# Output projection of an attention and expert block: two fp32 products against three fp32r products of high and low halves

## The chip, the cores and the metric

The kernel runs on one core of one Trainium2 chip. The metric is the device time of one execution in microseconds (us). Before the change it is 2347.66 us, the median of three runs (2343.93 to 2350.57). The engines are named as in the profile: PE is TensorE, PEld its weight loads, DVE VectorE, ACT ScalarE, POOL GpSimd, SP the engine that issues most DMAs.

## The reference

The input x has 16 blocks of 512 rows and 128 columns. The output is x + attention(xn) + experts(xn), where xn is the layer norm of x. The part that the change touches is the attention's last line:

```
new_vals = einsum('bhqk,bkhd->bqhd', softmax(q k^T), v)        # 16 heads of 64
out      = einsum('bqhe,hed->bqd', new_vals, w_out) + b_out
```

The expert part sends each row to the best two of 8 experts, each a two-layer network with silu, and adds the weighted results. Everything is in fp32, or as exact as three fp32r products of high and low halves make it.

## The kernel before, in words

All work is cut into groups G = 0, 1, 2, ... (256 that attend, and 6 more at the end). A pair of heads n (128 pairs: 16 blocks x 8) takes two groups, 2n and 2n+1: in each, PE makes the scores of two of its four row tiles (line 349), DVE takes the negated row maximum (line 355), ACT the exponential with its sum (line 360). One group later PE turns these tiles (line 372, four times four transposes) and DVE and ACT copy them from PSUM to PT (lines 384 and 382). In the middle of the four turns PE makes the next pair's K product (even groups) or Q product (odd groups), each as three fp32r products (helper `three`, lines 200 to 202); ACT casts its high half from PSUM (line 334) and DVE subtracts for the low half (line 335).

The later steps of a pair n are these. In group 2n+2 DVE takes the reciprocal of the row sums (line 406), PE turns it (line 411, called R below), DVE copies it (line 413) and two DMAs on SP write it to memory and read it back as the broadcast RB. In group 2n+3, as its last PE work, `weighted` makes the product with V (line 395, called PV), and DVE multiplies the result by RB into OT (line 401). In group 2n+4, for odd n, `project_out` multiplies the heads of the pairs n-1 and n by their parts of the output weights (lines 427 and 428, called OP), and DVE adds the result into acc (line 436). OT has four buffers. These OP groups are the ones with G%4 == 2; those with G%4 == 0 have two V products for the same or the next block in that place instead (`values`). After them in a group come R and the side work: the router of a block in the first half of the run (`router`, `logits`, `routed_rows` on POOL, and so on), and one expert tile in each three groups in the second half (from G = 138).

Order. Every engine runs its own queue, in an order fixed while the program is written: `add` puts an instruction with the names it needs into the group's open list, and `close` sorts DVE's and ACT's list by place. In DVE's list a group's places are max0, turn0, inverse, max1, low, turn1 and then everything else (side). In ACT's they are exp00, turn0, high, exp01, exp10, turn1, exp11, side. PE, POOL and SP keep the order in which the code adds.

Banks. Two pairs of PSUM banks hold the scores. Four more rotate (`xbank`), one for each other product in PE's order, and each use waits for the instruction that emptied the bank four uses earlier (`freed`). So in every group the third turned tile's bank, the K or Q product's bank and so on come back in a fixed rhythm.

The weights of the K, Q, V and router products are split into halves at the start by `split_weights` (ACT casts the high half, POOL or DVE subtracts). The output weights come by one DMA, whole, in fp32. RAW is a staging buffer for expert weights; its first use is in group 24.

Of the kernel before, what the change touches and what calls it, by code (L numbers as in the profile page):

```python
# [8 lines left out]
F32R = mybir.dt.float32r  # L9
# [6 lines left out]
P = 128  # L16
D = 128
# [12 lines left out]
WSPLIT = 24  # L30
DVE_ORDER = "max0 turn0 inverse max1 low turn1 side".split()
ACT_ORDER = "exp00 turn0 high exp01 exp10 turn1 exp11 side".split()
KQ_AT = 2
# [40 lines left out]
def block_kernel(nc, x, wq, wk, wv, wout, ns, bout, rw1, rb1, rw2, rb2, w1, w2, bias, ident, tri, consts, pick, out):  # L74
# [11 lines left out]
    with ExitStack() as ctx:  # L86
        def sb(name, shape, dt=F32, to=ctx):
            return to.enter_context(nc.sbuf_tensor(name, shape, dt))
# [10 lines left out]
        WV = sb("WV", [P, 2, H * DH], F32R)  # L99
        WO = sb("WO", [P, HP, D])  # L100
        RB2 = sb("RB2", [P, 1])
# [23 lines left out]
        RB = sb("RB", [P, 2, S])  # L125
        OT = sb("OT", [P, 4, S])
        acc = sb("acc", [P, QT, D])
# [89 lines left out]
        def stage_raw(n):  # L217
            src = (w1 if n < E else w2)[:, n % E * 512:(n % E + 1) * 512]
            add("sp", lambda e: e.dma_start(RAW[:, n % 2], src), needs=[("slo", n - 2)] if n >= 2 else [],
                name=("raw", n), step=16, sem=f"raw_{n % 2}")  # L220
# [166 lines left out]
        def weighted(n):  # L387
            b, p = divmod(n, HP)
            bk = xbank()

            def make(e):
                for k in range(QT):
                    for j in range(2):
                        h = 2 * p + j
                        m = e.matmul(bank[bk][j * DH:(j + 1) * DH, :], V[:, k, h * DH:(h + 1) * DH],  # L395
                                     PT[:, n % 2 * 2 + j, k, :], start=(k == 0), stop=(k == QT - 1))
                return m

            add("pe", make, needs=[("PT", n, QT - 1, 0), ("PT", n, QT - 1, 1), ("Vs", b, p // 4, QT - 1), ("Vs", b, p // 4, QT - 2),
                                   freed.get(bk)], name=("PV", n))  # L400
            add("dve", lambda e: e.tensor_tensor(OT[:, n % 4, :], bank[bk], RB[:, n % 2, :], ALU.mult),  # L401
                needs=[("PV", n), ("RB", n), ("OP", (n - 4) | 1) if n >= 4 else None], name=("OT", n))
            freed[bk] = ("OT", n)
# [5 lines left out]
        def spread(n):  # L409
# [10 lines left out]
                needs=[("rrow", n), ("OT", n - 2) if n >= 2 else None], name=("RB", n), step=16, sem=f"RB_{n % 2}")  # L420

        def project_out(n):
            b, p = divmod(n, HP)
            bk = xbank()

            def make(e):
                e.matmul(bank[bk], WO[:, p - 1, :], OT[:, (n - 1) % 4, :], start=True, stop=False)  # L427
                return e.matmul(bank[bk], WO[:, p, :], OT[:, n % 4, :], start=False, stop=True)  # L428

            add("pe", make, needs=[("OT", n), ("load", "wo"), freed.get(bk)], name=("OP", n))  # L430
            dst = acc[:].rearrange("p t d -> p (t d)")
# [345 lines left out]
        load("tri", TRI[:], tri)  # L777
        load("wo", WO[:].rearrange("p a b -> p (a b)"), wout)
        load("bo", BO[:], bout)
# [27 lines left out]
        split_weights("wq", wq_s, WQ, [1], DH ** -0.5, on="dve")  # L807
        split_weights("r1", r1_s, R1, [0])
        add("dve", lambda e: e.tensor_scalar(RB1H[:], RB1[:], 0.5, None, ALU.mult), needs=[("load", "rb1")], name=("rb1h",))
        add("dve", lambda e: e.memset(PM[:, 0, 0], 0.0), name=("pm0",))  # L810
# [136 lines left out]
        def group(G):  # L947
# [16 lines left out]
            if G % 2 == 0 and 1 <= G <= GROUPS:  # L964
                denominators(G // 2 - 1)
            halves_after(G)
            attending(G)
            if G % 2 == 0 and 1 <= G <= GROUPS:
# [86 lines left out]
```

How the kernel before makes its waits and increments, by code:

```python
    def emit(self, engine, eng, sems):  # L62
        seen = {}
        for make, needs, key, step in self.items[engine]:
            for sem, value in (self.value[n] for n in needs):
                if seen.get(sem, 0) < value:
                    eng.wait_ge(sems[sem], value)
                    seen[sem] = value
            ins = make(eng)
            if key is not None:
                ins.then_inc(sems[key], step)
# [915 lines left out]
        @block.sync  # L987
        def _(eng):
            q.emit("sp", eng, sems)
            for k, v in q.count.items():
                if k.startswith(("st_", "sadd", "spare_out", "base", "rrow", "tab", "b_tab", "sc_", "pads")):
                    eng.wait_ge(sems[k], v)
```

## Time and profile before

| | |
|---|---|
| median of three runs | 2347.66 us |
| the profiled execution's own time | 2347.15 us |
| its span, first to last instruction | 2345.3 us |
| mean granted TensorE clock | 0.983 of full speed |
| ACT busy | 1453.1 us (62%) |
| POOL busy | 952.1 us (41%) |
| line 427, OT by WO, 128 passes | 68.2 us busy |
| line 428, OT by WO, 128 passes | 66.4 us busy |
| line 401, OT, 128 | 88.1 us busy, 688 ns each |

How to read it: each of the 64 OPs has two fp32 matmuls, and each shows as two passes, so 256 passes in the two lines. A matmul's record is longer than the time until the next one may start, since matmuls are pipelined; the distance between starts is what PE spends. The same holds to a lesser degree for DVE and ACT. A wait is put down to the engine and line that came last.

### The profile page before, as it was taken

What the parts mean: (1) busy time and instruction counts of PE and PEld (TensorE: products, weight loads), DVE (VectorE), ACT (ScalarE), POOL (GpSimd) and SP (SyncE); (2) the same over time, 40 slices, a digit from 0 to 9 for tenths busy, and PEclk for the clock granted to TensorE, in tenths of its full rate; (3) what the DMA queues carried; (4) which work ended last, traced back from release to release, by engine and by line L of the source; (5) the groups of instructions that cost most, each with busy time, mean ns of one, the idle gap of its engine ahead of it and who ended that gap; (6) DMA issues with size and microseconds to landing.
All of it is one profiled execution on the core that took longest, in us unless ns stands there. A gap on an engine that the chain in (4) does not pass through costs nothing.

```text
span 2345.3 us, 36846 instructions
## 1 busy us (share of the span) xinstructions
PE 2199.6 (94%) x12720; PEld 1395.6 (60%) x12720; DVE 1752.8 (75%) x2908; ACT 1453.1 (62%) x3455; POOL 952.1 (41%) x793
## 2 busy tenths in 40 slices
PE   8999999999999999997999998999989989999997
PEld 5666566656666666654656665565656655656654
DVE  6777777777778878775777776777767767777775
ACT  5666666666666666654665665666666656666663
POOL 5333343544343433310145445445454354454353
PEclk8999999999999999998999999999999999999999
DMA  2122222211111010003133333323233223232232
GB/s 73 34 64 78 85 80 82 91 46 34 37 37 35 27 42 33 29 31 89 37 69 73 73 70 59 71 69 76 69 72 73 59 56 73 69 73 69 66 67 46
DMA packets 126856, 141.67 MB, mean 60 GB/s; under 512 B 18480, under 2 KB 93104, under 8 KB 126640
## 3 DMA queue, kind: packets, MB, share of 16 engines
q1 hardware_dynamic: 96080, 118.60, 16.2%
q0 software_dynamic: 30592, 20.73, 7.2%
q8 instruction: 102, 1.67, 0.3%
q14 instruction: 82, 0.67, 0.1%
HBM read 102.92 MB, written 38.46 MB: 60 GB/s over the span
## 4 chain that ended last, share of the span: by engine, by line
PE 47%; DVE 21%; DMA 12%; ACT 9%; issue 7%; POOL 2%; DVEq 0%; SPq 0%; ACTq 0%; POOLq 0%
PE bank L395 14%; PE pair L349 10%; DMA RB<-l_rows 9%; PE bank L372 8%; DVE NM L355 7%; DVE PT L384 3%; ACT PR L360 3%; DVE ZZ L709 2%; PE bank L427 2%; PE bank L428 2%; PE bank L200 2%; DMA l_rows<-RT 2%; ACT PT L382 2%; PE bank L720 2%; DVE QS L335 1%
## 5 line engine op out<-in xcount | busy, mean ns | idle before, releaser
L360 ACT ACTIVATE PR<-pair,NM 128x512 f32<-128x512 f32 x1024 | 715.0, 706 | 707.5 <-DVE NM L355 706.3
L355 DVE TENSOR_REDUCE NM<-pair 128x2 f32<-128x1024 f32 x512 | 617.3, 1206 | 135.2 <-PE pair L349 134.8
L372 PE MATMUL bank<-idn,PR 128*128 128x128 f32 x4096 | 560.7, 279 | 34.8 <-DVE PT L384 16.6
L372 PEld LDWEIGHTS bank<-idn,PR 128*128 128x128 f32 x4096 | 460.2, 142 | 181.5 <-issue 86.0
L395 PE MATMUL bank<-PT,V 128*64 128x512 f32 x2048 | 469.4, 600 | 15.4 <-ACT ZZ L700 8.7
L712 POOL TENSOR_TENSOR HH<-ZZ,HH 128x512 fp32r<-128x512 f32 x156 | 231.7, 1494 | 572.2 <-DVE HH L711 572.2
L349 PE MATMUL pair<-KS,QS 64*128 64x512 f32 x3072 | 435.6, 415 | 2.1 <-DVE QS L335 1.1
L349 PEld LDWEIGHTS pair<-KS,QS 64*128 64x128 f32 x3072 | 273.8, 187 | 190.1 <-issue 137.1
L384 DVE COPY PT<-bank 128x512 f32<-128x512 f32 x512 | 349.9, 683 | 18.5 <-PE bank L372 10.8
L382 ACT COPY PT<-bank 128x512 f32<-128x512 f32 x512 | 302.9, 592 | 8.5 <-PE bank L372 8.5
L395 PEld LDWEIGHTS bank<-PT,V 128*64 128x64 f32 x2048 | 136.2, 137 | 276.7 <-issue 230.6
L751 POOL DMA_INDIRECT out<-YS,IDW x156 | 245.0, 1571 | 71.1 <-issue 34.2
L489 POOL TENSOR_TENSOR TH<-TH,HS 128x512 f32<-128x512 f32 x64 | 82.2, 1285 | 460.0 <-ACT HS L486 459.7
L401 DVE TENSOR_TENSOR OT<-bank,RB 128x512 f32<-128x512 f32 x128 | 88.1, 688 | 239.9 <-PE bank L395 156.5
L360 ACT ACTIVATION_READ_ACCUMULATOR PR<-pair,NM 128x1 f32 x1024 | 221.7, 216 | 0.0
L592 POOL DMA_INDIRECT slots<-XR,IDX x128 | 124.7, 974 | 106.1 <-DVE junk L587 71.8
L709 DVE SCALAR_TENSOR_TENSOR ZZ<-ZT,ZZ 128x512 f32<-128x512 f32 x156 | 107.2, 687 | 76.6 <-ACT ZZ L700 76.4
L698 ACT ACTIVATE ZT<-bank,BT 128x512 f32<-128x512 f32 x156 | 110.6, 709 | 56.3 <-POOL HH L712 53.3
L711 DVE CAST HH<-ZZ 128x512 fp32r<-128x512 f32 x156 | 138.0, 884 | 5.4
L700 ACT ACTIVATE ZZ<-bank,BT 128x512 f32<-128x512 f32 x156 | 111.0, 711 | 0.0
L335 DVE TENSOR_TENSOR QS<-bank,QS 128x512 fp32r<-128x512 f32 x128 | 88.5, 691 | 16.3 <-ACT QS L334 13.9
L335 DVE TENSOR_TENSOR KS<-bank,KS 128x512 fp32r<-128x512 f32 x128 | 87.7, 685 | 14.8 <-ACT KS L334 14.4
(164 smaller groups left out, 2866.4 us busy)
## 6 DMA issues: line engine op xcount, KB each, us to landing
E<-w_tab SPq DMA_DIRECT2D x78, 512.0 KB, 7.3
RB<-l_rows SPq DMA_DIRECT2D x128, 256.0 KB
XG<-slots SPq DMA_DIRECT2D x39, 264.0 KB, 7.4
w_tab<-SPL SPq DMA_DIRECT2D x16, 512.0 KB, 4.8
xin<-in_x SPq DMA_DIRECT2D x16, 256.0 KB, 7.7
XQ<-in_x SPq DMA_DIRECT2D x16, 256.0 KB, 6.9
RAW<-in_w SPq DMA_DIRECT2D x16, 256.0 KB, 7.9
slots<-PAD SPq DMA_DIRECT2D x15, 264.0 KB, 5.1
```

The source lines that it names most:

```text
L335: add("dve", lambda e: e.tensor_tensor(lo, bank[bk], hi, ALU.subtract), needs=[(name + "hi", n), *old], name=(name + "lo", n), place="low")
L349: m = e.matmul(bank[bk + j], a[half[j], cols], c[half[j], :], start=(k == 0), stop=(k == 2))
L355: add("dve", lambda e: e.tensor_reduce(NM[:, 2 * t:2 * t + 2], pairs[t % 2][:], AX.X, ALU.max, negate=True), needs=[("S", n, t), ("exp", n ...
L360: add("act", lambda e: e.activation(PR[:, k, :], bank[t % 2 * 2 + j], ACT.Exp, bias=NM[:, k:k + 1], accum_out=RS[:, n % 2, j, t:t + 1]), n ...
L372: m = e.transpose(bank[bk][:, c * P:(c + 1) * P], PR[:, k, c * P:(c + 1) * P], idn[:])
L382: add("act", lambda e: e.copy(dst, src), needs=[("T", n, t, j), *old], name=("PT", n, t, j), place=f"turn{t % 2}")
L384: add("dve", lambda e: e.tensor_copy(dst, src), needs=[("T", n, t, j), *old], name=("PT", n, t, j), place=f"turn{t % 2}")
L395: m = e.matmul(bank[bk][j * DH:(j + 1) * DH, :], V[:, k, h * DH:(h + 1) * DH], PT[:, n % 2 * 2 + j, k, :], start=(k == 0), stop=(k == QT - 1))
L709: add("dve", lambda e: e.scalar_tensor_tensor(ZZ[:, r], ZT[:, r], 1.0, ZZ[:, r], ALU.add, ALU.mult), needs=[("zt", n), ("zz", n)], name=(" ...
L711: add("dve", lambda e: e.tensor_copy(hi, ZZ[:, r]), needs=[("s", n), old], name=("hi", n))
L712: add("pool", lambda e: e.tensor_tensor(lo, ZZ[:, r], hi, ALU.subtract), needs=[("hi", n), old], name=("lo", n))
L751: add("pool", lambda e, t=t: e.indirect_dma_start(out, bass.IndirectOffsetOnAxis(ap=IDW[:, i % 4, t, 0:1].bitcast(U32), axis=0), YS[:, i % ...
```

## The change

The output weights WO and the normalised heads OT are each kept as a high fp32r half and a low half (the rest). The heads now go from PSUM to an fp32 buffer OF, of which there is one; then ACT casts the high half and DVE subtracts for the low half (`halve_heads`), at new places called heads: first in ACT's order and between inverse and max1 in DVE's. Both run in group 2n+4, in every even group. OT has two buffers for each half. An OP is six fp32r matmuls (low weights by high heads, high by high, high by low, for each of two pairs) where it was two fp32 matmuls. The weights come by two DMAs into RAW at the start and are split there by ACT and POOL; the first two expert weights wait for that before they use RAW.

```diff
-DVE_ORDER = "max0 turn0 inverse max1 low turn1 side".split()
-ACT_ORDER = "exp00 turn0 high exp01 exp10 turn1 exp11 side".split()
+DVE_ORDER = "max0 turn0 inverse heads max1 low turn1 side".split()
+ACT_ORDER = "heads exp00 turn0 high exp01 exp10 turn1 exp11 side".split()
...
-        WO = sb("WO", [P, HP, D])
+        WO = sb("WO", [P, 2, HP * D], F32R)
...
-        OT = sb("OT", [P, 4, S])
+        OF = sb("OF", [P, S])
+        OT = sb("OT", [P, 2, 2, S], F32R)
...
-            add("sp", lambda e: e.dma_start(RAW[:, n % 2], src), needs=[("slo", n - 2)] if n >= 2 else [],
+            add("sp", lambda e: e.dma_start(RAW[:, n % 2], src), needs=[("slo", n - 2) if n >= 2 else ("wlo", "wo", n)],
...
-            add("dve", lambda e: e.tensor_tensor(OT[:, n % 4, :], bank[bk], RB[:, n % 2, :], ALU.mult),
-                needs=[("PV", n), ("RB", n), ("OP", (n - 4) | 1) if n >= 4 else None], name=("OT", n))
+            add("dve", lambda e: e.tensor_tensor(OF[:], bank[bk], RB[:, n % 2, :], ALU.mult),
+                needs=[("PV", n), ("RB", n), ("OTl", n - 1) if n else None], name=("OT", n))
...
+        def halve_heads(n):
+            old = [("OP", (n - 2) | 1)] if n >= 2 else []
+            add("act", lambda e: e.copy(OT[:, n % 2, 0], OF[:]), needs=[("OT", n), *old], name=("OTh", n), place="heads")
+            add("dve", lambda e: e.tensor_tensor(OT[:, n % 2, 1], OF[:], OT[:, n % 2, 0], ALU.subtract),
+                needs=[("OTh", n), *old], name=("OTl", n), place="heads")
...
-                e.matmul(bank[bk], WO[:, p - 1, :], OT[:, (n - 1) % 4, :], start=True, stop=False)
-                return e.matmul(bank[bk], WO[:, p, :], OT[:, n % 4, :], start=False, stop=True)
-
-            add("pe", make, needs=[("OT", n), ("load", "wo"), freed.get(bk)], name=("OP", n))
+                for k in (p - 1, p):
+                    hi, lo = OT[:, k % 2, 0], OT[:, k % 2, 1]
+                    wh, wl = (WO[:, j, k * D:(k + 1) * D] for j in range(2))
+                    e.matmul(bank[bk], wl, hi, start=(k < p), stop=False)
+                    e.matmul(bank[bk], wh, hi, start=False, stop=False)
+                    m = e.matmul(bank[bk], wh, lo, start=False, stop=(k == p))
+                return m
+
+            add("pe", make, needs=[("OTl", n), ("wlo", "wo", 0), ("wlo", "wo", 1), freed.get(bk)], name=("OP", n))
...
-        load("wo", WO[:].rearrange("p a b -> p (a b)"), wout)
+        for c in range(2):
+            load(f"wo{c}", RAW[:, c], wout[:, c * 512:(c + 1) * 512])
...
+        split_weights("wo", RAW[:].rearrange("p a b -> p (a b)"), WO, [0, 1])
...
+            if G % 2 == 0 and 0 <= G - 4 < GROUPS:
+                halve_heads(G // 2 - 2)
             attending(G)
```

## Rows read from the trace of the kernel before

**Rows 1.** The page's part 1, busy time of each engine over the whole span.
```profile
PE 2199.6 (94%) x12720; PEld 1395.6 (60%) x12720; DVE 1752.8 (75%) x2908; ACT 1453.1 (62%) x3455; POOL 952.1 (41%) x793
```

**Rows 2.** The page's part 4, shares of the chain that ended last.
```profile
PE 47%; DVE 21%; DMA 12%; ACT 9%; issue 7%; POOL 2%; DVEq 0%; SPq 0%; ACTq 0%; POOLq 0%
```

**Rows 3.** Who waited for whom, whole span: us in total, times, longest us.
```profile
ACT PR L360 <- DVE NM L355: 706.3, 214, 6.4
...
DVE OT L401 <- DMA RB<-l_rows: 83.4, 39, 8.5
...
PEld bank L200 <- DVE KS L335: 31.0, 64, 1.9
...
PEld pair L349 <- ACT PR L360: 7.8, 21, 1.3
```

**Rows 4.** Timeline, routing half, G%4 == 2: start us, duration us, engine, line.
```profile
608.17 1.67 PE L349 MATMUL pair<-KS,QS 64*128 64x512 f32 x12
...
610.45 0.69 ACT L360 ACTIVATE PR<-pair,NM 128x512 f32<-128x512 f32 x1 [4.76 <-DVE NM L355]
...
611.07 0.19 DVE L406 RECIPROCAL RI<-RS 128x8 f32<-128x8 f32 x1
...
612.27 1.02 PE L427 MATMUL bank<-OT,WO 128*128 128x512 f32 x2
612.27 0.68 DVE L335 TENSOR_TENSOR KS<-bank,KS 128x512 fp32r<-128x512 f32 x1
...
612.87 0.68 DVE L384 COPY PT<-bank 128x512 f32<-128x512 f32 x1
...
613.99 0.27 PE L411 MATMUL bank<-idn,RI 128*8 128x128 f32 x1
...
614.02 0.47 PE L200 MATMUL bank<-XT,R 128*128 128x512 f32 x1
...
614.19 0.69 DVE L436 TENSOR_TENSOR acc<-bank,acc 128x512 f32<-128x512 f32 x1 [0.64 <-PE bank L428]
...
614.33 0.39 PE L201 MATMUL bank<-XT,R 128*128 128x512 f32 x1
...
614.56 0.40 PE L202 MATMUL bank<-XT,R 128*128 128x512 f32 x1
...
624.75 0.69 DVE L401 TENSOR_TENSOR OT<-bank,RB 128x512 f32<-128x512 f32 x1 [1.58 <-DMA RB<-l_rows]
```

**Rows 5.** Instructions of lines 225, 709 and 579: ns min/median/max, first and last start us.
```profile
L225 ACT CAST SPL<-RAW x16: 632/638/680, 234.1 to 474.9; 128x512 fp32r<-128x512 f32 x16
```
```profile
L709 DVE SCALAR_TENSOR_TENSOR ZZ<-ZT,ZZ x156: 678/688/693, 1133.5 to 2305.7; 128x512 f32<-128x512 f32 x156
```
```profile
L579 DVE TENSOR_TENSOR gt<-gt x32: 179/188/1194, 94.6 to 1044.6; 128x32 f32<-128x32 f32 x32
```

**Rows 6.** Timeline, routing half, a group with G%4 == 0.
```profile
177.36 1.04 POOL L265 TENSOR_TENSOR XR<-XR,sqo 128x512 f32<-128x512 f32 x1
...
178.14 0.19 DVE L406 RECIPROCAL RI<-RS 128x8 f32<-128x8 f32 x1
...
179.43 0.69 DVE L335 TENSOR_TENSOR KS<-bank,KS 128x512 fp32r<-128x512 f32 x1
...
180.18 0.50 PE L200 MATMUL bank<-WV,HT 128*128 128x512 f32 x1 [0.25 <-DVE KS L335]
...
181.19 1.83 PE L349 MATMUL pair<-KS,QS 64*128 64x512 f32 x12
```

**Rows 7.** Timeline, expert half, a group with G%4 == 2.
```profile
1700.62 0.68 DVE L384 COPY PT<-bank 128x512 f32<-128x512 f32 x1
...
1701.67 0.48 PE L720 MATMUL bank<-HH,E 128*128 128x512 f32 x1
```

**Rows 8.** Timeline, the last output projection of the run.
```profile
2334.96 0.69 DVE L401 TENSOR_TENSOR OT<-bank,RB 128x512 f32<-128x512 f32 x1 [8.47 <-DMA RB<-l_rows]
...
2335.71 2.08 PE L427 MATMUL bank<-OT,WO 128*128 128x512 f32 x2 [6.21 <-DVE OT L401]
```

## The prediction, made before the changed kernel was run

> **What bounds the kernel now.** I read the page's busy shares first, then its chain of waits, then the totals of who waited for whom, then a few microseconds of the timeline in each kind of group.
>
> TensorE (PE) is busy 94% of the span and VectorE (DVE) 75% [rows 1]. The chain that ended last is 47% PE and still 21% DVE [rows 2]. So PE leads, but at some place in each round it is let go by DVE. The waits name the place: the weight load of line 200 (a V product) waited 64 times for DVE's KS, the low half of K that line 335 writes [rows 3]. ScalarE (ACT) is the loose engine: it waited 706.3 us in 214 pieces for the row maximum [rows 3].
>
> The groups G come in fours. In those with G%4 == 2 PE's order after the score products is T, T, K product, T, T, output projection (OP), R (the small turn of the inverse sums), then the next stage's product. In those with G%4 == 0 it is T, T, K product, T, T, V product, V product, R. Four banks rotate, so the second V product takes the K product's bank, which line 335 empties; after an OP it is R that takes that bank, and the product behind R takes the bank of the third T, which a DVE copy (line 384) empties. That copy is DVE's next instruction behind line 335.
>
> **Part by part.**
>
> *The OP on PE.* Today its two fp32 products are four passes. The first starts at 612.27 and R at 613.99: 1.72 us [rows 4]. Three fp32r products of the same width start at 614.02, 614.33 and 614.56, so 0.31 us for the first of a block and 0.23 us for each later one [rows 4]. Six of them take 0.31 + 5 x 0.23 = 1.46 us. PE is given 0.26 us per OP, 64 x 0.26 = 16.6 us in all, if nothing else holds it. No new bank is taken.
>
> *The cast on ACT.* 128 casts at the head of each even group. The nearest row, an fp32r copy from SBUF, has 638 ns [rows 5]. It waits for OT, which stands on DVE just before the first maximum. ACT is idle there for 4.76 us in the sample group, waiting for that maximum [rows 4], and the maximum takes 1.2 us behind OT. The cast ends first; behind it on ACT stands only the exponential that waits for that same maximum. Its cost is 0. Were ACT late, it would be 0.6 us per even group (up to 77 us); the 706.3 us of waits say it is not.
>
> *The subtraction on DVE.* 128 of them, put between the reciprocal and the second maximum in every even group. Its row is bounded by the 688 ns of a 512-wide operation with two SBUF inputs [rows 5], but instructions of DVE overlap a little: line 335 starts at 612.27 and line 384 behind it at 612.87 [rows 4]. So one more in the stream costs 0.60 us. From there on the second maximum, line 335 and line 384 are all 0.60 us later. What each does to PE:
>
> - G%4 == 0: line 335 ends at 179.43 + 0.69 = 180.12 and the V product starts at 180.18, released by it [rows 6]. That wait is there in each such group (64 in [rows 3]); no slack. 62 groups with two V products and the new subtraction x 0.60 = 37.2 us on PE. Everything behind it (R, the scores of the next group) moves along, and DVE's side work is late by the same 0.60, so nothing later takes it back, with two exceptions below.
> - G%4 == 2: R has slack, for line 335 ends at 612.95 and R starts at 613.99. The product behind R doesn't have enough: the copy of line 384 ends at 613.55, the product starts at 614.02 [rows 4]; with the 0.06 us that a release takes it could start at 613.61. With the copy at 614.15 it starts at 614.21, 0.19 late, though OP ended early. In a group of the expert stage the copy ends at 1701.30 and the product starts at 1701.67 [rows 7]; there it comes 0.29 late. So OP's 0.26 us are given away to a wait for the bank, and more: with 31 such groups in each half of the run, 31 x 0.19 + 31 x 0.29 = 14.9 us. DVE's own lateness ends there, since acc waits 0.64 us for OP anyway [rows 4]. The bounds are -0.26 (if the copy isn't late) and +0.60 (if DVE's lateness reaches PE whole).
> - OP itself needs the subtraction's result. It ends some 0.7 us behind the reciprocal (611.26), at 611.95, and OP starts at 612.27 [rows 4]: covered, with 0.3 us left.
>
> *What takes some back.* DVE's OT waited 39 times for the broadcast RB [rows 3], in the routing half as at 624.75, at the start of a G%4 == 0 group [rows 4]. That DMA starts from R's copy in the G%4 == 2 group, behind acc, and these hardly move; so the 0.19 us of that group shorten the wait instead: 31 x 0.19 = -5.9 us. And the scores behind a G%4 == 0 group in the routing half take 1.83 us where others take 1.67 [rows 4, 6], held by the last exponential, 21 times in [rows 3]. ACT slips less than PE, so this bubble closes: 21 x 0.16 = -3.4 us.
>
> *POOL.* The subtraction reads two SBUF tensors. Line 579, a small instruction (128x32) of that kind that often falls beside a POOL tensor operation, has a median of 188 ns and a maximum of 1194 [rows 5]; I read the 1 us more as a wait for such a POOL operation. In the sample group POOL's line 265 runs from 177.36 to 178.40, across the end of the reciprocal at 178.33, and line 266 (as long) follows [rows 6]. This is the group in which routed_rows puts its three POOL tensor operations, 15 in the run. Between 0 and 1.04 us each, taken at the middle: 15 x 0.5 = +7.5 us, on the path, since these are G%4 == 0 groups. In the expert half POOL does indirect DMAs at that place; line 709, two SBUF inputs too, has a maximum of 693 ns in 156 [rows 5], so nothing is added there.
>
> The Trainium skill, "SBUF — State Buffer", section "Who interferes with whom", says that a VectorE instruction with two SBUF inputs contends with a GpSimd one that reads SBUF and that the later of the two is blocked whole. Line 579's maximum agrees [rows 5]. By that rule alone a subtraction that starts just after line 266 would wait all of its 1.04 us, 15.6 us in all in place of 7.5.
>
> *The start.* wout goes as two transfers into RAW, one issue of about 0.5 us more on SP behind everything urgent; two casts more on ACT, two subtractions more on POOL. ACT's first exponential waits for a maximum behind other DVE work, POOL is idle later, and the first user of RAW (the expert weights, G = 24) and of WO (G = 6) are far off. Cost 0, at most 1.2 us (two casts).
>
> *The end.* The last OT starts at 2334.96 behind its DMA and OP at 2335.71 follows at once [rows 8]. Here cast and subtraction stand bare: 0.64 + 0.69 + 0.1 for two releases = 1.4 us. TensorE runs at its lower clock there (two passes 2.08 us, against 0.86 apart in mid run), so OP gives back about 0.5. Net +0.9 us.
>
> **The sum.** 37.2 + 14.9 - 5.9 - 3.4 + 7.5 + 0.9 = +51.2 us. The profiled execution took 2347.15 us (span 2345.3), 0.5 us under the median of the runs shown (2347.66). 2347.15 + 51.2 = 2398.
>
> **Rivals.**
>
> 1. *PE sets the pace and DVE's idle time (2345.3 - 1752.8 = 592.5 us) covers the subtraction* (faster). For it: 94% against 75% [rows 1]. Against it: that idle time lies in front of OT and of the first maximum, not between the reciprocal and line 335, where the 64 waits of line 200 are. Its place is that bank; it decides if the V product's wait for line 335 is under 0.26 us per group on average after the change. Then 64 x -0.26 + 0.9 = -15.7: 2331 us.
> 2. *Half of it.* The G%4 == 2 groups keep OP's 0.26 us (the bank behind R not binding), the others lose 0.60: 37.2 - 16.6 - 3.4 + 0.9 = +18, with POOL's share up to +26: about 2368.
> 3. *DVE is the bound in all even groups:* 0.60 us lost in each of 125: 75 + 7.5 + 0.9 - 3.4 = +80: 2427. For it: chains in the expert half run through five DVE instructions in a row. Against it: acc's wait for OP, in which DVE's lateness ends.
> 4. *The fp32r products of OP don't go at 0.23 us*, the change not doing what it says: at the passes' 0.43 us six take 2.6 us, +0.86 per OP, 55 us on top of 37: about 2440. Against it: every fp32r product in [rows 4].
>
> **How the numbers follow.** Forecast (2398, own range 2380 to 2415) 0.63; rival 3 0.14; rival 2 0.12; rival 1 0.07; rival 4 0.04. The predicted time is 2398. The range takes in rivals 2 and 3 with a little beyond each: 2362 to 2432, leaving out rivals 1 and 4 and some of the tails. About 0.3% (7 us) is what a measurement can tell from no change. Faster 0.07 (rival 1), same 0.04 (the lower end of rival 2), slower 0.89.
>
> **What would show it.** Right: OP to R 1.46 us; the wait of line 200's V product for KS up from 0.5 to about 1.1 us each; a new wait of the product behind R for line 384's copy; ACT's wait for the maximum down by the casts; the subtraction about 0.69 us, over 1 us in some 15 groups. Groups with G%4 == 0 longer by 0.4 to 0.6 us, G%4 == 2 by 0.2 to 0.3, odd ones unchanged. Wrong: an unchanged wait for KS, or even groups no longer than before (rival 1); odd groups longer (rival 3, or ACT as the bound).

## The result

The changed kernel takes 2398.75 us (median of 4 runs, 2396.14 to 2404.33), the kernel before 2349.01 us (median of 4). The ratio is 1.0214, 95% interval 1.0198 to 1.023. The forecast was 2398. The profiled execution took 2396.78 us, its span is 2395.0 us, 49.7 us more than before.

### The profile after

The lines named here are 1 to 12 further down than before: the scores are L350, the maximum L356, the K low half L336, the V product L201, OT is now OF at L402, the cast L425, the subtraction L426, the projection's three products L437 to L439, R L412, acc L448.

The page's busy times and the shares of the chain that ended last (against [rows 1] and [rows 2]):

```profile
PE 2192.8 (92%) x12848; PEld 1424.0 (59%) x12848; DVE 1829.4 (76%) x3036; ACT 1546.4 (65%) x3585; POOL 960.9 (40%) x795
```
```profile
PE 40%; DVE 34%; issue 10%; ACT 8%; DMA 5%; POOL 1%; DVEq 0%; SPq 0%; ACTq 0%; POOLq 0%
```

PE is busy for 7 us less, and DVE's share of the chain has gone from 21% to 34%. That is the whole case in two lines: the engine that got less work isn't the one that lets the groups go.

Who waited for whom (us in total, times, longest), against [rows 3]:

```profile
ACT OT L425 <- DVE OF L402: 357.7, 109, 11.2
ACT PR L361 <- DVE NM L356: 303.4, 227, 6.2
...
PEld bank L201 <- DVE KS L336: 69.3, 64, 2.6
...
DVE OF L402 <- DMA RB<-l_rows: 45.3, 16, 4.2
```

The V product's wait for the K low half is 69.3 us where it was 31.0, in the same 64 places: 0.60 us more in each. ACT's 706.3 us of waiting for the maximum are now split between the cast's wait for OF and the maximum. The wait for RB fell from 83.4 us in 39 places to 45.3 us in 16. Five more waits of the same multiplication, 21.0 us, stand under "issue", with no releaser found; the last of them (9.45 us, below) was put down to RB before (8.47 us). With these five it is 66.3 us in 21 places, a fall of 17 us.

The timeline of the group with G%4 == 2 whose form before is in [rows 4] (start us, duration us, engine, line):

```profile
619.63 1.66 PE L350 MATMUL pair<-KS,QS 64*128 64x512 f32 x12
...
620.47 0.62 ACT L425 CAST OT<-OF 128x512 fp32r<-128x512 f32 x1 [3.33 <-DVE OF L402]
...
621.89 0.69 ACT L361 ACTIVATE PR<-pair,NM 128x512 f32<-128x512 f32 x1 [0.80 <-DVE NM L356]
...
622.62 0.64 DVE L426 TENSOR_TENSOR OT<-OF,OT 128x512 fp32r<-128x512 f32 x1
...
623.18 1.22 DVE L356 TENSOR_REDUCE NM<-pair 128x2 f32<-128x1024 f32 x1
...
623.64 0.48 PE L437 MATMUL bank<-OT,WO 128*128 128x512 f32 x1
...
624.32 0.68 DVE L336 TENSOR_TENSOR KS<-bank,KS 128x512 fp32r<-128x512 f32 x1
...
624.91 0.68 DVE L385 COPY PT<-bank 128x512 f32<-128x512 f32 x1
...
625.15 0.27 PE L412 MATMUL bank<-idn,RI 128*8 128x128 f32 x1
...
625.51 0.68 DVE L448 TENSOR_TENSOR acc<-bank,acc 128x512 f32<-128x512 f32 x1
...
625.65 0.50 PE L201 MATMUL bank<-XT,R 128*128 128x512 f32 x1 [0.24 <-DVE PT L385]
```

The projection takes 625.15 - 623.64 = 1.51 us (1.72 before). But the product behind R (625.65) starts 6.02 us after the scores (619.63), where it was 614.02 - 608.17 = 5.85: 0.17 later. It is let go by L385, whose copy ends at 625.59. PE's saving turned into a wait for a bank. The cast ends at 621.09, ahead of the exponential that waits for the maximum.

A group with G%4 == 0 in the routing half, against [rows 6]:

```profile
180.33 0.62 ACT L425 CAST OT<-OF 128x512 fp32r<-128x512 f32 x1 [3.21 <-DVE OF L402]
...
182.05 0.64 DVE L426 TENSOR_TENSOR OT<-OF,OT 128x512 fp32r<-128x512 f32 x1
...
182.14 1.45 POOL L267 TENSOR_TENSOR XR<-XR,sqo 128x512 f32<-128x512 f32 x1
...
183.74 0.68 DVE L336 TENSOR_TENSOR KS<-bank,KS 128x512 fp32r<-128x512 f32 x1
...
184.47 0.50 PE L201 MATMUL bank<-WV,HT 128*128 128x512 f32 x1 [0.74 <-DVE KS L336]
...
185.47 1.66 PE L350 MATMUL pair<-KS,QS 64*128 64x512 f32 x12
```

PE's idle time ahead of the V product is 0.74 us (0.25 before). POOL's L267 started behind the subtraction and took 1.45 us, where the same operation had taken 1.04: here DVE came first. The scores behind take 1.66 us in place of 1.83, so that bubble closed, as forecast.

The cast and the subtraction over the run (ns min/median/max, first and last start us):

```profile
L425 ACT CAST OT<-OF x128: 615/621/626, 52.1 to 2385.3; 128x512 fp32r<-128x512 f32 x128
```
```profile
L426 DVE TENSOR_TENSOR OT<-OF,OT x128: 632/642/1412, 54.2 to 2385.9; 128x512 fp32r<-128x512 f32 x128
```

The end of the run, against [rows 8]:

```profile
2384.55 0.69 DVE L402 TENSOR_TENSOR OF<-bank,RB 128x512 f32<-128x512 f32 x1 [9.45 <-issue]
...
2385.93 0.69 DVE L426 TENSOR_TENSOR OT<-OF,OT 128x512 fp32r<-128x512 f32 x1 [0.68 <-ACT OT L425]
...
2386.67 0.80 PE L437 MATMUL bank<-OT,WO 128*128 128x512 f32 x1 [8.64 <-DVE OT L426]
...
2389.64 0.69 DVE L448 TENSOR_TENSOR acc<-bank,acc 128x512 f32<-128x512 f32 x1 [3.02 <-PE bank L439]
```

From OF's start to acc's start it takes 5.09 us, where it was 2339.53 - 2334.96 = 4.57 before. Cast and subtraction put 2386.67 - 2384.55 = 2.12 us between OF and the projection (0.75 before), and the projection gives 0.85 us back.

### By kind of group

A group's length is the time from its first score weight load to the next group's, read from each trace. Summed over the routing half (31 groups of each kind, G = 4 to 127) and the expert half (28 or 29 of each, G = 140 to 254), the difference to the kernel before in us:

```
                         routing half, G%4 =       expert half, G%4 =
                          0     1     2     3       0     1     2     3
changed                  +7.5  +1.5  +8.8  +0.1   +11.6  +5.9  +6.5  +2.5
no halving               -2.6  +0.2  -9.3  -0.2    +0.3  +2.9  -8.1  +6.1
no halving, again        -4.4  +0.1 -10.0  -0.1    -0.1  +0.1  -8.1  +9.1
cast only, again         -4.6   0.0  -9.3  -0.2     0.0  +1.5  -7.8 +10.5
fp32 and halving        +15.7  +1.5  +8.2   0.0   +12.9  +5.9 +10.6  -0.1
even pairs late         -12.0  +9.2 +13.7   0.0    +5.6  +4.8  +6.9  +1.6
on POOL                 +10.6   0.0  -9.0  -0.2    -1.3  +2.1 +156.5 -20.9
projection a group later -19.0 +7.7 -22.9 +52.8    +3.4  +5.9 -26.8 +44.4
same, POOL for even     -19.3  +8.9 -23.1 +50.1    -2.4  +3.7 -27.3 +45.9
in DVE's wait           +16.7  +1.6 -27.9  +4.1   +28.4  -5.8 -16.7 +18.2
mixed                    +5.9  +9.5  -5.2  -0.1    +0.2  +1.5  +8.8  +2.6
two subtractions        +46.7 +18.0 +25.1  +6.4   +29.9  +5.5 +27.0  +1.3
```

The changed kernel's line gives 44.4 us; 2.8 lie in the 12 groups between the halves, 1.1 at the end and 1.3 before G = 4.

Not all of this is waiting. The profile shows TensorE's granted clock at its full level (2.4 GHz) through the routing half in both kernels, but at the lower level (1.2 GHz) for 34.1 us of the expert half before the change and for 51.2 us after it. The expert half repeats itself every 12 groups (a tile takes three groups, two pairs take four), and the extra low stretches lie in the groups with G%12 == 4 and the ones behind them. There PE stands idle for a DVE copy, 2.47 or 2.48 us in each of the nine such groups before and 2.75 us after; before, the clock was low somewhere in these two groups in four cases out of nine, after it in all nine. G = 220, before (clock full) and after. The last line is a stretch of the profile; its third number from the end is the granted clock (1.00 is full, 0.50 the lower level). The score products take 2.82 us there in place of 1.66:

```profile
1977.24 0.66 PE L737 MATMUL bank<-idn,YT 128*128 128x128 f32 x4 [2.48 <-DVE V L317]
1977.82 1.66 PE L349 MATMUL pair<-KS,QS 64*128 64x512 f32 x12
```
```profile
2014.73 1.04 PE L749 MATMUL bank<-idn,YT 128*128 128x128 f32 x4 [2.75 <-DVE V L318]
2015.70 2.82 PE L350 MATMUL pair<-KS,QS 64*128 64x512 f32 x12
2014.90:2018.30 3.40, 3.40 (x16) 2.28 (x15) 2.17 (x3) 0.00 (x0) 2.19 (x3) 0.50 0.07 8
```

The nine groups with G%12 == 5 show the price: together they have 13.9 us more at the low level and are 6.2 us longer, 0.45 us for each. That is all of the 5.9 us that the expert half's G%4 == 1 groups grew by, and at this price the half's 17.1 us more are about 8 us (an estimate) of the 49.7. The 1.3 us before G = 4 are of this kind too: in every kernel here that is 1 us or more later at that point, the cast-only ones among them, the clock is low for 3.4 us from about 28 us on, and in no other.

### The profile page after: what moved, and what is told of

The parts are those of the page before. It is cut to its first block, busy times and chain, and to the rows that moved or that the text cites. A ratio compares the mean times of both kernels' runs of the same rounds, so it can differ in the third digit from the quotient of the medians.

```text
span 2395.0 us, 37489 instructions
## 1 busy us (share of the span) xinstructions
PE 2192.8 (92%) x12848; PEld 1424.0 (59%) x12848; DVE 1829.4 (76%) x3036; ACT 1546.4 (65%) x3585; POOL 960.9 (40%) x795
## 4 chain that ended last, share of the span: by engine, by line
PE 40%; DVE 34%; issue 10%; ACT 8%; DMA 5%; POOL 1%; DVEq 0%; SPq 0%; ACTq 0%; POOLq 0%
PE bank L396 14%; PE pair L350 10%; DVE NM L356 10%; DVE PT L385 7%; PE bank L373 5%; DMA RB<-l_rows 4%; DVE ZZ L721 3%; DVE OT L426 3%; DVE KS L336 3%; ACT PR L361 2%; PE bank L732 2%; PE bank L201 2%; DVE HH L723 2%; ACT PT L383 2%; PE bank L734 1%
## 5 line engine op out<-in xcount | busy, mean ns | idle before, releaser
L356 DVE TENSOR_REDUCE NM<-pair 128x2 f32<-128x1024 f32 x512 | 622.6, 1216 | 146.2 <-PE pair L350 145.9
L350 PE MATMUL pair<-KS,QS 64*128 64x512 f32 x3072 | 437.3, 417 | 2.3 <-DVE QS L336 1.2
L350 PEld LDWEIGHTS pair<-KS,QS 64*128 64x128 f32 x3072 | 277.7, 190 | 187.8 <-issue 137.8
L385 DVE COPY PT<-bank 128x512 f32<-128x512 f32 x512 | 349.7, 683 | 18.5 <-PE bank L373 10.5
L425 ACT CAST OT<-OF 128x512 fp32r<-128x512 f32 x128 | 79.5, 621 | 358.0 <-DVE OF L402 357.7
L402 DVE TENSOR_TENSOR OF<-bank,RB 128x512 f32<-128x512 f32 x128 | 88.1, 688 | 230.8 <-PE bank L396 164.5
L361 ACT ACTIVATION_READ_ACCUMULATOR PR<-pair,NM 128x1 f32 x1024 | 215.6, 211 | 0.0
L201 PE MATMUL bank<-WV,HT 128*128 128x512 f32 x128 | 62.8, 491 | 42.6 <-DVE KS L336 41.2
```

The source lines that it names most:

```text
L350: m = e.matmul(bank[bk + j], a[half[j], cols], c[half[j], :], start=(k == 0), stop=(k == 2))
L356: add("dve", lambda e: e.tensor_reduce(NM[:, 2 * t:2 * t + 2], pairs[t % 2][:], AX.X, ALU.max, negate=True), needs=[("S", n, t), ("exp", n ...
L361: add("act", lambda e: e.activation(PR[:, k, :], bank[t % 2 * 2 + j], ACT.Exp, bias=NM[:, k:k + 1], accum_out=RS[:, n % 2, j, t:t + 1]), n ...
L385: add("dve", lambda e: e.tensor_copy(dst, src), needs=[("T", n, t, j), *old], name=("PT", n, t, j), place=f"turn{t % 2}")
```

## The experiments

The theory: DVE's subtraction makes the banks of the K product and of the third turned tile free later, PE waits for these banks, and so even the time that the projection gives back is lost. The rivals: the halving's cost and the projection's gain just add up; DVE's load as such sets the time; the cast is what costs. Ratios are to the kernel before on the same chip, which had medians of 2349.7, 2344.8 and 2345.4 us in the three sets.

### The two parts apart

The changed kernel without any halving:

```diff
-            add("dve", lambda e: e.tensor_tensor(OF[:], bank[bk], RB[:, n % 2, :], ALU.mult),
+            add("dve", lambda e: e.tensor_tensor(OT[:, n % 4, :], bank[bk], RB[:, n % 2, :], ALU.mult),
...
-                    hi, lo = OT[:, k % 2, 0], OT[:, k % 2, 1]
+                    hi, lo = OT[:, (n - p + k) % 4, :], OL[:]
```

> The changed kernel without the halving: the multiplication by RB writes the fp32r heads itself, and the low half of the heads is a tile of zeros, so the third product adds nothing (the low half of the heads is left out of the result). PE does the same six fp32r products. Bank theory: with no subtraction ahead, the projection's shorter time is passed on whole: 64 x 0.21 to 0.26 = 13 to 17 us under before, 2332 to 2337. Rival (PE's time in the projection is hidden anyway, or six weight loads cost something else): 2346 to 2350.

Measured: 2331.67 us, ratio 0.9917 (0.9896 to 0.9939). Again on another chip:

> The kernel without any halving once more, beside the one with the cast alone on the same chip, to price the cast. Expected 0.991 to 0.994 of before.

Measured: 2328.26 us, ratio 0.9928 (0.9912 to 0.9943). The shorter projection is worth 17 to 18 us. In both halves the G%4 == 2 groups are 0.3 us shorter each, but only the routing half keeps it: in the expert half the groups behind them (G%4 == 3) give 6 to 9 us back, and that half as a whole takes 1173.1 and 1172.8 us against 1171.9 before. In the second of the two traces, 3.4 of the 9.1 us lie in the ten groups with G%12 == 11, 0.33 us in nearly each: PE has come there earlier and waits longer for DVE to empty the banks of acc and of a turned tile. 6.6 us lie in two groups (151 and 199) with 10.2 us at the low clock, which had none before. The wait for the K low half is that of before:

```profile
PEld bank L202 <- DVE KS L337: 30.7, 64, 2.2
```

So the rival by which PE's time in the projection is hidden falls.

The kernel before with the halving beside it:

```diff
+            add("act", lambda e: e.copy(OH[:, 0], OT[:, n % 4, :]), ..., name=("OTh", n), place="heads")
+            add("dve", lambda e: e.tensor_tensor(OH[:, 1], OT[:, n % 4, :], OH[:, 0], ALU.subtract), ..., place="heads")
...
-            add("pe", make, needs=[("OT", n), ("load", "wo"), freed.get(bk)], name=("OP", n))
+            add("pe", make, needs=[("OTl", n), ("load", "wo"), freed.get(bk)], name=("OP", n))
```

> The kernel before (fp32 output projection, whole weights), plus the cast and the subtraction of the change at the change's places, into a tile that no product reads; the projection waits for the subtraction as in the change. Bank theory: behind a projection PE waits for the third tile's copy in either case, so the longer fp32 passes (1.72 us against 1.51) cost nothing extra and the time is that of the changed kernel within 4 us: 2396 to 2403. Rival (additive: the halving costs 63 us and the shorter projection really gives 64 x 0.21 = 13 us back): 2410 to 2416.

Measured: 2403.65 us, ratio 1.0227 (1.0208 to 1.0247), against 1.0214 (1.0198 to 1.023) for the changed kernel. The additive rival asked for 11 to 17 us (0.5% to 0.7%) over the changed kernel; the medians show 0.13%, and the two intervals leave room for about half of it. So it falls as stated, but the gain isn't lost whole. The wait for K's low half is the changed kernel's, the wait for RB isn't (96.0 us in 39 places; 66.3 in 21 there, with those under "issue"):

```profile
DVE OT L402 <- DMA RB<-l_rows: 96.0, 39, 8.6
...
PEld bank L201 <- DVE KS L336: 69.3, 64, 2.6
```

The longer projection makes R later, RB lands later, and the G%4 == 0 groups of the routing half wait for it (+15.7 us against +7.5; this profiled execution, span 2405.0, is 10 us longer than the changed kernel's). So behind R the gain is lost to the bank, as forecast (+8.2 and +8.8 us in the G%4 == 2 groups), and what R brings forward reaches RB.

The cast alone (no subtraction, the low half zeros), and again beside the kernel without halving:

```diff
-            add("dve", lambda e: e.tensor_tensor(OT[:, n % 2, 1], OF[:], OT[:, n % 2, 0], ALU.subtract),
-                needs=[("OTh", n), *old], name=("OTl", n), place="heads")
```

> The changed kernel with the cast on ACT but without the subtraction on DVE (the low half of the heads is zeros, left out of the result). Bank theory: the cast lies in ACT's wait for the first maximum and costs nothing on the path, so the time is that of the kernel without any halving (2332) within 4 us. Rival (the cast and the hand-over between engines carry part of the cost): 2340 or more.

Measured: 2335.86 us, ratio 0.996 (0.9949 to 0.9972).

> The kernel with the cast alone once more, on the chip of the one without halving. If the cast is free but for the run's end (about 0.7 us bare there), it stands within 2 us of that one; if the 4 to 10 us that the earlier two runs differ by are real, 4 us or more above it.

Measured: 2335.7 us, ratio 0.9961 (0.9947 to 0.9975), beside 0.9928 (0.9912 to 0.9943) on the same chip. The kernel with the cast is 7.4 us longer by the medians. The traces (spans 2333.5 and 2327.9 us) place 3.3 us of it in the expert half, 0.3 in the routing half, 0.3 at the end, 0.5 between the halves and 1.4 before G = 4. But the cast delays no group: the 222 groups of both halves that ran at full clock in both traces differ by 0.1 us in sum. The expert half's 3.3 us lie in 17 groups with low clock in one of the two (51.2 us against 44.4 in that half), and the 1.4 us at the start are the low stretch told of above; the late-even kernel has the same cast and neither that stretch nor the 1.4 us. If the cast moves these stretches, or how, no run shows. Its price remains small beside the subtraction, which takes the kernel from 0.996 to 1.021.

### Where the subtraction stands

The even pairs' subtraction behind the third tile's copy:

```diff
-DVE_ORDER = "max0 turn0 inverse heads max1 low turn1 side".split()
+DVE_ORDER = "max0 turn0 inverse heads max1 low turn1 late side".split()
...
-                needs=[("OTh", n), *old], name=("OTl", n), place="heads")
+                needs=[("OTh", n), *old], name=("OTl", n), place="heads" if n % 2 else "late")
```

> The changed kernel, with the subtraction of the even pairs (the groups with G%4 == 0) behind the third turned tile's copy instead of ahead of the second maximum. These low halves are needed only two groups later. DVE does as much work as in the changed kernel. Bank theory: in these groups the V product no longer waits longer for the K low half, so its summed wait goes back from 69 to about 31 us, and most of the 27 us by which the G%4 == 0 groups and the ones behind them grew comes back: 2370 to 2380 us against 2399. Rival (DVE's load as such sets the time, wherever the subtraction stands): 2395 to 2402.

Measured: 2382.94 us, ratio 1.0139 (1.0123 to 1.0154). 16 us come back, so the place counts and DVE's load as such isn't the whole; but I expected 19 to 29. The G%4 == 0 groups of the routing half got 19.5 us shorter, and the ones behind them 7.7 us longer and the G%4 == 2 ones 4.9: DVE's lateness is paid one and two groups on. In G = 21 the Q low half comes 0.33 us later than before the change and the product behind it waits 0.50 us in place of 0.18. R's copy there starts 1.32 us into the group, where it was 0.11, so the transfer of RB starts later, and in the G%4 == 2 groups of that half the multiplication waits for RB 59.6 us in 16 places, against 31.1 in 9 in the changed kernel.

All subtractions on POOL:

```diff
-            add("dve", lambda e: e.tensor_tensor(OT[:, n % 2, 1], OF[:], OT[:, n % 2, 0], ALU.subtract),
-                needs=[("OTh", n), *old], name=("OTl", n), place="heads")
+            add("pool", lambda e: e.tensor_tensor(OT[:, n % 2, 1], OF[:], OT[:, n % 2, 0], ALU.subtract),
+                needs=[("OTh", n), *old], name=("OTl", n), place="side")
```

> The changed kernel with all subtractions on POOL in place of DVE, ahead of the group's other POOL work. DVE is as free as before the change. Bank theory: in the routing half the groups with a projection get shorter by 0.21 to 0.26 us each, about -7 us; in the expert half POOL's queue (four indirect DMAs of 1.57 us per tile, each set waiting for the one before to land) makes the low half late for the projection in some of the 30 projections there, by some us each. 2340 to 2375, most likely 2350. Rival (the cast on ACT, not the subtraction, is what costs): no gain against the changed kernel, 2395 to 2400 or more.

Measured: 2484.51 us, ratio 1.0572 (1.0554 to 1.059): a miss by over 100 us. In the routing half the G%4 == 2 groups did what was expected (-9.0 us), but the G%4 == 0 ones grew by 10.6 us, which I hadn't forecast. In the expert half 23 of the 29 projections wait for POOL, 1.6 to 10.6 us each. Its waits, and its POOL queue in one stretch:

```profile
PEld bank L437 <- POOL OT L426: 139.8, 24, 10.8
```
```profile
1756.07 1.58 POOL L763 DMA_INDIRECT out<-YS,IDW  x1
1757.95 1.56 POOL L763 DMA_INDIRECT out<-YS,IDW  x1 [0.30 <-issue]
1758.96 1.85 POOL L426 TENSOR_TENSOR OT<-OF,OT 128x512 fp32r<-128x512 f32 x1
```

The subtraction stands behind indirect DMAs and what they wait for. I had named the queue and priced it far too low, and left the clock out: PE's idle time there goes with 174 us at the low level in the expert half, against 51 in the changed kernel. At 0.45 us each these 123 us are some 55 of the 110 us that this half is longer than in the changed kernel (an estimate).

The projection a group later, with all subtractions late on DVE; and the same with the even pairs' subtractions of the expert half on POOL:

```diff
-            n = (G - 4) // 2
-            if G % 4 == 2 and 1 <= n < PAIRS:
+            n = (G - 5) // 2
+            if G % 4 == 3 and 1 <= n < PAIRS:
                 project_out(n)
```

> The changed kernel with every subtraction behind the third turned tile's copy, and the output projection one group later (G%4 == 3), so that it never waits for it. DVE's work is unchanged. Bank theory: no bank in the groups with G%4 == 2 or 0 comes free later than before the change, and the shorter projection is passed on; what stays is DVE's lateness carried into the group behind each G%4 == 0 one, 15 to 20 us as in the kernel with the late even half. 2345 to 2365, most likely 2355. Rival (DVE's load as such): 2383 or more, as with the late even half.

> As the kernel with the projection one group later, but from group 138 on (the expert half) the even pairs' subtractions are on POOL, where they may be late by a group without holding anyone. Against that kernel: DVE's 0.56 us per G%4 == 0 group of the expert half go away, 30 x 0.3 to 0.5 = 9 to 15 us: 2335 to 2352. Rival (the cost in the expert half isn't DVE's): no difference.

Measured: 2399.23 us, ratio 1.0226 (1.02 to 1.0252), and 2395.33 us, ratio 1.0217 (1.02 to 1.0234). Both miss. The table shows why: the G%4 == 2 groups lose 31.7 us against the changed kernel in the routing half (1.02 us each), the G%4 == 3 ones gain 52.7 (1.70 each; 1.43 in the 26 that had full clock). The projection costs its whole time in its new group,

```profile
629.82 0.48 PE L437 MATMUL bank<-OT,WO 128*128 128x512 f32 x1
...
631.06 0.40 PE L439 MATMUL bank<-OT,WO 128*128 128x512 f32 x1
631.39 3.65 PE L396 MATMUL bank<-PT,V 128*64 128x512 f32 x16
```

while in the G%4 == 2 group it partly filled a hole in which PE waits for DVE's banks. POOL for the even pairs is worth 7 us in the expert half by the traces (I expected 9 to 15), but the two medians' intervals overlap.

The subtraction at the end of the odd group, ahead of the next multiplication, with the projection in the G%4 == 0 group:

```diff
+            if G % 2 and 0 <= G - 5 < GROUPS:
+                low_heads((G - 5) // 2)
             if G % 2 and 0 <= G - 3 < GROUPS:
                 weighted((G - 3) // 2)
```

> The same halving with the subtraction moved to the one place where DVE is idle in most groups: at the end of the odd group, ahead of the next pair's multiplication, which waits for the V product or for RB. The projection moves to the G%4 == 0 group, ahead of its two V products. If the place decides and not DVE's load, the subtraction costs next to nothing and the shorter projection counts: 2325 to 2345, most likely 2335; the wait of the V product for the K low half (31 us) goes away, a like one comes in the G%4 == 2 groups. Rival (DVE's load as such): 2370 or more.

Measured: 2374.6 us, ratio 1.0132 (1.0114 to 1.0149). A miss: 40 us over what I thought most likely, 30 over the range. It isn't for the subtraction's sake in the G%4 == 1 groups (+1.6 and -5.8 us, the latter with 15 us less at the low clock than before). In the expert half's G%4 == 3 groups (+18.2) and with the projection moved into the G%4 == 0 groups (+16.7 and +28.4) the price is paid again. Of the +18.2, 8.3 us lie in the 25 groups that had full clock in both traces, the rest in three that had not. Two things were changed at once, so their shares in the expert half stay open.

Each place where it was cheapest:

```diff
+            odd, routing = n % 2 == 1, 2 * n + 4 < FIRST
+            on, place = ("pool", "side") if odd == routing else ("dve", "late" if routing else "heads")
```

> The changed kernel with each half of each stage where its cost was least so far. Routing half: the odd pairs' subtraction (needed at once by the projection) on POOL, the even pairs' on DVE behind the third tile's copy. Expert half: the odd pairs' on DVE where the change has it, the even pairs' on POOL. Adding the group sums of the runs so far against before (-9 for G%4 == 2 in the routing half, -3 for G%4 == 0 and 1 there, +1 for them and +9 for G%4 == 2 and 3 in the expert half, +1 at the end): about -1, so 2342 to 2356, no worse than before and some 48 us under the changed kernel. If instead the load of the halving as such costs what it does in the change: 2385 or more.

Measured: 2372.61 us, ratio 1.0115 (1.0097 to 1.0133). 26 us under the changed kernel, the best with the full result, and still slower than before. The group sums don't add: with the G%4 == 2 groups shorter (-5.2), the G%4 == 0 groups of the routing half have +5.9 where the late-even kernel had -12.0. 4.3 of the 5.9 us lie in two groups in which the clock was low (for 3.8 us in all). In the others RB seems to be in the way: the scores start at 178.34, the multiplication at 180.15. The profile finds no releaser for it, but by then the low half of the pair before (166.32) and the product with V were done, and of what it needs only RB was open.

```profile
178.34 1.65 PE L350 MATMUL pair<-KS,QS 64*128 64x512 f32 x12
...
180.15 0.69 DVE L402 TENSOR_TENSOR OF<-bank,RB 128x512 f32<-128x512 f32 x1 [2.33 <-issue]
```

### A second subtraction

```diff
+            add("dve", lambda e: e.tensor_tensor(OJ[:], OF[:], OT[:, n % 2, 0], ALU.subtract),
+                needs=[("OTh", n)], name=("OTm", n), place="heads")
```

> The changed kernel with a second, equal subtraction behind the first (into a tile that nothing reads). Bank theory: the first one used up the slack behind the projection, so the second costs its whole 0.56 us in every even group, 0.56 x 125 = 70 us: 2460 to 2472. Rival (a shared loss, DVE's idle time taking part of every added instruction): the second costs no more than the first did, some 50 to 60 us: 2448 to 2458.

Measured: 2514.75 us, ratio 1.0728 (1.0711 to 1.0746): 116 us over the changed kernel, not 70. The direction of the theory is right (the second costs more than the first), the total isn't.

```profile
L429 DVE TENSOR_TENSOR OJ<-OF,OT x128: 677/685/1530, 53.4 to 2503.0; 128x512 fp32r<-128x512 f32 x128
```
```profile
ACT PR L362 <- DVE NM L357: 414.0, 338, 6.9
...
PEld bank L202 <- DVE KS L337: 119.1, 64, 3.5
...
PE bank L413 <- DVE KS L337: 30.8, 60, 1.6
```

ACT now waits for the second maximum too (338 waits in place of 227), and R waits for the K low half.

The groups tell where the 116 us lie, against the changed kernel. In the 97 even groups that ran at full clock in both traces the second subtraction costs 0.60 us in the median, 0.55 to 0.65 us in 82 of them; the 92 odd groups of that kind are unchanged (median 0.00). So the bank theory's price holds group by group, and 0.60 x 125 = 75 us of it. 15 of the second subtractions started while a POOL tensor operation had 0.98 us to go and took 1.52 to 1.53 us, 12.6 us more than the others in all. And the granted clock, which was full through the changed kernel's routing half, is low there for 64.8 us here (0.97 over the stretch below, where the changed kernel has 1.00; the V product is that of G = 68, behind a wait of 2.93 us):

```profile
615.97 0.79 PE L202 MATMUL bank<-WV,HT 128*128 128x512 f32 x1 [2.93 <-DVE KS L337]
...
70.00:1020.00 950.00, 867.73 (x5180) 557.17 (x5179) 757.19 (x1457) 601.53 (x1437) 355.28 (x329) 0.97 0.15 49
```

PE's wait for the K low half in the groups with G%8 == 4 of that half is 0.47 to 1.24 us in the changed kernel, and the clock fell behind none of the 16; it is 1.35 to 3.02 us here, and the clock fell at 14 of the 16. The odd groups behind them (G%8 == 5) have 36.9 us at the low level and are 16.6 us longer, 0.45 us for each again. At that price the 64.8 us cost 29 us, and 75 + 12 + 29 = 116 us (an estimate). I had left the clock out of the forecast of 70.

## Why the prediction was right

Point by point, by its own steps:

- *OP on PE*: 1.46 us forecast, 1.51 measured. That the gain is real without the halving, and that with it the G%4 == 2 groups are as long with either form of the projection in the routing half, is shown by the two kernels that have one part of the change each. I had missed that R itself, 0.2 us earlier, brings RB forward, and that the projection is not always covered: in eight groups (four in the routing half: 30, 46, 94 and 118) its first weight load waits 0.26 to 0.38 us for the subtraction. In those four OF had waited for RB.
- *G%4 == 0*: the K low half late by 0.60 us, its wait up by 38.3 us over 64 places against 37.2 forecast. Right in place and size. But "no slack, everything behind moves along" was wrong in the expert half: at full clock the groups with G%12 == 0 grew by 0.28 us, those with G%12 == 8 by 0.20, and only the one with G%12 == 4 that had full clock in both traces grew by 0.61. In G = 144 the V product is 0.59 us later, the product behind R only 0.28: before the change it started 0.11 us behind the end of ACT's copy of the fourth turned tile, whose bank it takes (1189.77 and 1189.88), and now that copy is done in time.
- *The refunds*: they came. In the routing half's G%4 == 0 groups the wait for RB fell from 47.3 us in 30 places to 14.3 in 8 (those under "issue" taken in), and the exponential's bubble closed (the groups with G%8 == 5 are 0.17 us shorter). Not forecast: the groups with G%8 == 1 of that half are 0.3 us longer, since DVE's side work of the group before slips into them, and the wait for RB grew in G%4 == 2 (13.8 to 31.1 us). Forecast for the routing half's G%4 == 0 and 1 groups, with POOL's share: 31 x 0.60 - 5.9 - 3.4 + 7.5 = 16.8 us. Measured: 9.0.
- *The expert half's G%4 == 0 and 1*: 29 x 0.60 = 17.4 us forecast, 17.5 measured, and this agreement is luck. By the classes above, waiting accounts for some 10 to 11 us (an estimate), about 7 less than forecast; as much again came from the low clock, a term that the prediction had put at nothing.
- *G%4 == 2*: +0.19 us forecast for the routing half, 0.28 measured. In 27 of the 31 groups it was 0.18 to 0.27 (median 0.21), whatever product follows R; in the four named above it was 0.70 to 0.88. Expert half: 9.0 us forecast, 6.5 + 2.5 measured in G%4 == 2 and 3.
- *POOL*: 7.5 us forecast for 15 collisions. In 13 groups the subtraction was lengthened by a POOL tensor operation that was running, and these 13 took 5.6 us more than the others' 0.65 in all. The term is real and was a little high. In the trace DVE also came first at times, and then POOL's operation got longer.
- *The cast*: forecast 0. In the groups it is 0; the kernel with the cast is 7.4 us longer by the medians (5.6 by the spans), and what the traces place of that in the halves and at the start goes with low clock.
- *The clock*: not in the sum, about 8 us in the expert half and 1.3 at the start. My sign "odd groups unchanged" failed in the expert half, where they grew by 8.4 us; 5.9 of it, the G%4 == 1 groups, is the clock.
- *The end*: +0.9 forecast, +0.5 between OF and acc, +1.1 from the last group's start.

So the sum of 51.2 us hit 49.7 with errors of some 15 us in each direction: the G%4 == 0 groups of both halves too high, the clock, the routing half's G%4 == 2 groups and the groups between the halves (2.8 us) too low. The mechanism was shown by the experiments; that the number is so close is luck.

Rival 1 (DVE's idle time covers it) and rival 4 fall by the KS wait and by the 1.51 us. Rival 2 (the G%4 == 2 groups keep the projection's gain) falls by their +8.8 and +6.5 us. Rival 3 would have had DVE's 0.60 us in all even groups; it doesn't hold for the first subtraction, but it is what the second one costs.

## What to carry to other kernels

An engine that is busy 94% of the time needn't pass on a saving: see if what follows waits for a buffer that another engine frees, and look up, for the instruction right behind the saved one, how long its buffer had been free. The price of an added instruction is set by its place in the queue: read the slack of each consumer behind it, group kind by group kind, and take a sample in each stage. Slack is spent once: sums of separately measured gains and the price of a second like instruction don't follow from the first. And a wait can cost more than its length: compare the granted clock stage by stage, not only over the span, since longer idle times of PE were followed by stretches at the lower clock.

## What I had not expected of the hardware

One extra DVE instruction of 642 ns with two SBUF inputs costs the stream 0.56 us (622.62 to 623.18), and up to 1412 ns when a POOL tensor operation that reads SBUF is running. The length then follows from what POOL has left: in the 12 cases of the changed kernel with more than 0.15 us left, and in all 15 of the second subtraction, it ended 0.54 to 0.56 us behind the POOL operation. Beside POOL's indirect DMAs alone it was not longer in the changed kernel (at most 708 ns).

The granted clock hardly shows in the mean (0.981 after, 0.983 before) and yet has a price: 0.45 us for each us at the lower level in the groups where it could be read alone. In the kernels without any halving the expert half has 44 to 48 us at the low level, with 34 before; if the projection's form as such does that, no run shows.
